# Reordering the norm loop, and changing how weight loads are guarded and cut, in a transformer layer on 8 cores

## The reference

```python
x = L0_attn_x                                   # [8, 4096, 1024] fp32
xn = _layernorm(x)
x = x + attention(xn) + ffn(xn)

# attention: 8 heads of 256, key and value from a latent of rank 64
q = xn @ Wq.T;  kv = xn @ Wkv_down.T
k = kv @ Wk_up.T;  v = kv @ Wv_up.T
out = softmax(q k^T / 16) v @ Wo.T

# ffn: weights rounded to {-1, 0, 1} by the mean of |w|, activations to 8 bits per token
gate = silu(bitlinear(xn, w_gate));  up = bitlinear(xn, w_up)       # 1024 -> 4096
y = bitlinear(gate * up, w_down)                                     # 4096 -> 1024
```

## Time and profile before

| what | value |
|---|---|
| runs | 5657.88, 6039.49 (median), 6048.05 us |
| the profiled execution | 5657.88 us, its span 5656.3 us (slowest core, core 6; cores 5638.6 to 5656.3) |
| granted PE clock | 0.890 to 0.891 of full speed on all cores |
| norm loop | 0 to 758 us |
| attention | 758 to 3491 us: PE busy 2314.15 us |
| first hole | 3491 to 3651 us: PE busy 12.87 us |
| up and gate | 3651 to 4862 us |
| second hole | 4862 to 5008 us: PE busy 28.78 us |
| down | 5008 to 5656 us: PE busy 636.40 of 648 us |
| busy over the span | PE 74%, DVE 37%, ACT 38%, POOL 12% |

### The profile page before, as it was taken

One profiled execution on the slowest core, in us unless ns is written; L12 is line 12 of the kernel. 1 busy time (PEld: TensorE's weight loads), 2 busy tenths in 40 slices (PEclk: granted clock), 3 DMA queues, 4 the chain that ended last, 5 costly groups with the idle time before them and its releaser, 6 DMA issues.

```text
span 5656.3 us, 93209 instructions; the slowest of 8 cores (5638.6 to 5656.3 us)
## 1 busy us (share of the span) xinstructions
PE 4170.3 (74%) x23803; PEld 2339.4 (41%) x24244; DVE 2077.0 (37%) x2817; ACT 2163.8 (38%) x3587; POOL 664.0 (12%) x643
## 2 busy tenths in 40 slices
PE   1222379798897987979879796288888888279999
PEld 1111246455453554635546363144333433134444
DVE  5434621211212112121121211099999999301111
ACT  3322456364563645636456363033333333100000
POOL 1110000000000000000000000133333333000000
PEclk9999689899898998979989898699999999589999
DMA  5454421011010110101101212111111111245553
GB/s 130 128 127 121 121 62 42 25 42 46 22 42 25 42 46 22 42 25 42 46 21 44 83 44 66 37 31 36 38 38 31 36 38 36 72 135 130 131 131 105
DMA packets 532527, 350.66 MB, mean 62 GB/s; under 512 B 441824, under 2 KB 482784, under 8 KB 532000
## 3 DMA queue, kind: packets, MB, share of 16 engines
q1 hardware_dynamic: 467856, 155.24, 11.9%
q0 software_dynamic: 51248, 164.26, 10.3%
q10 hardware_dynamic: 12896, 25.17, 1.3%
HBM read 244.61 MB, written 109.05 MB: 63 GB/s over the span
## 4 chain that ended last, share of the span: by engine, by line
PE 54%; DVE 23%; issue 9%; DMA 6%; ACT 5%; SPq 1%; DVEq 1%; POOLq 1%; ACTq 0%; POOL 0%
PE psF L710 17%; PE psF L699 15%; PE psF L997 8%; PE psF L383 4%; DVE rsc L461 4%; DVE t L452 3%; DVE rsc L458 3%; PE psF L983 3%; DVE arB L464 2%; PE psF L875 2%; DVE smf L900 2%; PE psF L881 2%; ACT arB L723 1%; DVE rsc L455 1%; PE psT L760 1%
## 5 line engine op out<-in xcount | busy, mean ns | idle before, releaser
L704 ACT ACTIVATE arB<-psF 128x512 bf16<-128x512 f32 x2048 | 1210.1, 597 | 695.0 <-PE psF L699 459.7
L710 PE MATMUL psF<-arB 128*128 128x257 bf16 x8192 | 1271.7, 281 | 135.7 <-ACT arB L704 133.9
L699 PE MATMUL psF<-arB 128*128 128x512 bf16 x3841 | 1192.0, 393 | 34.9 <-DVE arB L426 20.7
L710 PEld LDWEIGHTS psF<-arB 128*128 128x128 bf16 x8192 | 788.2, 100 | 559.7 <-issue 196.6
L875 PE MATMUL psF<-arA,arB 128*128 128x512 bf16 x1958 | 518.4, 406 | 94.5 <-DMA arB<-xnqT_d 85.1
L881 PE MATMUL psF<-arB 128*128 128x512 bf16 x2042 | 485.0, 380 | 62.3 <-DMA arB<-wuT_d 62.0
L997 PE MATMUL psF<-arB,arA 128*128 128x512 bf16 x2009 | 447.9, 381 | 82.7 <-DMA arB<-wdT_d 80.7
L896 POOL TENSOR_TENSOR arC<-arC 128x512 f32<-128x512 f32 x256 | 417.9, 1632 | 770.2 <-ACT arC L893 770.2
L699 PEld LDWEIGHTS psF<-arB 128*128 128x128 bf16 x4096 | 412.1, 101 | 112.4 <-issue 29.1
L719 DVE RECIPROCAL smf<-psF 128x1 f32<-128x1 f32 x256 | 43.1, 168 | 1128.7 <-PE psF L710 1108.0
L888 ACT ACTIVATE arC<-psF,smf 128x512 f32<-128x512 f32 x256 | 175.7, 686 | 635.2 <-PE psF L881 635.2
(11 more groups left out here) (130 smaller groups left out, 3601.6 us busy)
## 6 DMA issues: line engine op xcount, KB each, us to landing
arC<-Wg POOLq DMA_DIRECT2D x64, 512.0 KB, 5.5
arC<-Wu POOLq DMA_DIRECT2D x64, 512.0 KB, 5.8
arC<-Wd POOLq DMA_DIRECT2D x64, 512.0 KB, 5.7
hqT_d<-p1b SPq DMA_DIRECT2D x32, 1024.0 KB, 6.2
arA<-hqT_d SPq DMA_DIRECT2D x32, 1024.0 KB, 9.5
arC<-x SPq DMA_DIRECT2D x32, 512.0 KB, 4.9
aoT_d<-arB SPq DMA_DIRECT2D x64, 256.0 KB, 2.1
arC<-x ACTq DMA_DIRECT2D x32, 512.0 KB, 6.1
```

The costliest lines, as they stand in the source:

```text
L699: p.add("tensor", lambda e, bi=bi, c=c, g=g, d2=d2: e.matmul(bank(g), kT[:, d2 * T + c * 128: d2 * T + (c + 1) * 128], qT[:, d2 * T + bi * ...
L704: p.add("scalar", lambda e, g=g, c=c: e.activation(pT[c % 3][:, :], bank(g), AF.Exp, bias=0.0, scale=ISCL), reads=[b_bank[g]], writes=[b_p ...
L710: p.add("tensor", lambda e, c=c, sub=sub: e.matmul(pv_ps(sub, 0, 257), pT[c % 3][:, sub * 128:(sub + 1) * 128], vA[:, c * 257:(c + 1) * 25 ...
```

## The change

Seven edits:

- In the norm loop `emit_xnq_out`, `emit_passA` and `emit_prep_tile` move from the end of the iteration to before x's transposes; the kv product becomes a function (`emit_kv`) and is done one iteration later, also before x's transposes. The k and v groups of head 0 therefore start one chunk later.
- The very last aoT_d store uses buffer 0 of `aoTh` instead of 1.
- The first two xnqT_d loads are guarded by kvT and `aoTh[1]` alone.
- Each wuT_d slice is loaded in two pieces of 256 columns, the first by ACT, the second by POOL; the up product waits for both.
- In up and gate all four transpose groups stand behind the eight slices.
- wdT_d is loaded in eight 1 MB pieces, and a down matmul waits for its own piece.
- The guard lists are rebuilt for the new buffers.

```diff
+            if tc >= 1:
+                emit_xnq_out(tc - 1)
+            for j in range(3 * tc, min(3 * tc + 3, len(passA))):
+                emit_passA(j)
+            for _ in range(3):
+                emit_prep_tile()
+            if tc >= 1:
+                emit_kv(tc - 1)
             tb = nb()
             (x's eight transposes)
             (copy into arA)
-            (eight kv matmuls of tc, copy into kvT)
-            if tc >= 1:
-                emit_xnq_out(tc - 1)
             round5(xn32[:, :], b_xn, p1b[:, bb * 1024:(bb + 1) * 1024], rq, sxv, b_sxv)
-            for j in range(3 * tc, min(3 * tc + 3, len(passA))):
-                emit_passA(j)
-            for _ in range(3):
-                emit_prep_tile()
         emit_xnq_out(NTC - 1)
+        emit_kv(NTC - 1)
...
-                    if pre_k and 4 * pre_k[0][1] + 3 < tc:
+                    if pre_k and 4 * pre_k[0][1] + 4 < tc:
...
-                    if pre_v and pre_v[0] < tc:
+                    if pre_v and pre_v[0] + 1 < tc:
...
-                pb = bi % 2
+                pb = 0 if (h == NH - 1 and bi == 7) else bi % 2
...
-        b_wu8 = [Buf() for _ in range(8)]
+        b_wu8h = [[Buf(), Buf()] for _ in range(8)]
+        xnq_guard = b_kvT.handover() + b_aoTh[1].handover()
...
         for isl in range(8):
-            tok = p.add("scalar" if isl % 2 == 0 else "gpsimd", (load 512 columns),
-                reads=[b_d["wuT"]], writes=[b_wu8[isl]], extra=guard_wu, dma=True)
+            for hf in range(2):
+                c0 = isl * 512 + hf * 256
+                tok = p.add("scalar" if hf == 0 else "gpsimd", (load 256 columns from c0),
+                    reads=[b_d["wuT"]], writes=[b_wu8h[isl][hf]], extra=guard_wu, dma=True)
...
-                extra=((guard_wu + ao_guard) if tc < 2 else ()), dma=True)
+                extra=(xnq_guard if tc < 2 else ()), dma=True)
...
-                        reads=[b_xnqst[bb], b_wu8[isl]], writes=[b_bank[gu]])
-                if tc >= 1 and isl in (6, 7):
-                    emit_trans_group(tc - 1, isl - 6)
+                        reads=[b_xnqst[bb], b_wu8h[isl][0], b_wu8h[isl][1]],
+                        writes=[b_bank[gu]])
...
-                emit_trans_group(tc - 1, 2)
-                emit_trans_group(tc - 1, 3)
+                for g_ in range(4):
+                    emit_trans_group(tc - 1, g_)
...
         for n_ in range(2):
-            p.add("gpsimd", (load 32 x 512 columns of wdT_d),
-                reads=[b_d["wdT"]], writes=[b_wd2[n_]], extra=guard_wd, dma=True)
+            for q_ in range(4):
+                p.add("gpsimd", (load 8 x 512 columns, rows q_ * 8 on),
+                    reads=[b_d["wdT"]], writes=[b_wd2[n_][q_]], extra=guard_wd, dma=True)
...
-                        reads=[b_hqst[bb], b_wd2[n_]], writes=[b_bank[dbk[n_]]])
+                        reads=[b_hqst[bb], b_wd2[n_][ic // 8]],
```

More of the change, by code:

```diff
@@ L513, in emit_xnq_out, with emit_kv @@
                 reads=[rs2], writes=[b_d["xnqT"]], dma=True)
+        def emit_kv(tc2):
+            for dc in range(NDC):
+                p.add("tensor", lambda e, dc=dc, tc2=tc2: e.matmul(
+                    bank(0)[0:LR, 0:128], wkvT[:, dc * LR:(dc + 1) * LR],
+                    xnT_sl(dc, tc2 * 128, 128),
+                    start=(dc == 0), stop=(dc == NDC - 1)),
+                    reads=[b_wkvT, b_arA], writes=[b_bank[0]])
+            p.add("vector", lambda e, tc2=tc2: e.tensor_copy(
+                kvT[:, tc2 * 128:(tc2 + 1) * 128], bank(0)[0:LR, 0:128]),
+                reads=[b_bank[0]], writes=[b_kvT])
         pre_q = [(oc_, ts__) for ts__ in range(8) for oc_ in range(2)]
@@ L807, in build_nc @@
         for isl in range(8):
[L808 to L813 removed]
+            for hf in range(2):
+                c0 = isl * 512 + hf * 256
+                tok = p.add("scalar" if hf == 0 else "gpsimd",
+                            lambda e, c0=c0: e.dma_start(
+                    out=arB[:, 0:32768].rearrange("pp (dc i) -> pp dc i", i=NI)[:, :, c0:c0 + 256],
+                    in_=wuT_d.rearrange("(dc pp) i -> pp dc i", pp=128)[:, :, c0:c0 + 256]),
+                    reads=[b_d["wuT"]], writes=[b_wu8h[isl][hf]],
+                    extra=guard_wu, dma=True)
             tok_wu = tok
@@ L924, in build_nc @@
         emit_hq_dma(NTC - 1)
-        b_wd2 = [Buf(), Buf()]
+        b_wd2 = [[Buf() for _ in range(4)], [Buf() for _ in range(4)]]
         b_wo2 = [Buf(), Buf()]
@@ L956, in build_nc @@
         for n_ in range(2):
-            p.add("gpsimd", lambda e, n_=n_: e.dma_start(
-                out=arB[:, 0:32768].rearrange("pp (ic n) -> pp ic n", n=D)[:, :, n_ * 512:(n_ + 1) * 512],
-                in_=wdT_d.rearrange("(ic pp) n -> pp ic n", pp=128)[:, :, n_ * 512:(n_ + 1) * 512]),
-                reads=[b_d["wdT"]], writes=[b_wd2[n_]],
-                extra=guard_wd, dma=True)
+            for q_ in range(4):
+                p.add("gpsimd", lambda e, n_=n_, q_=q_: e.dma_start(
+                    out=arB[:, 0:32768].rearrange("pp (ic n) -> pp ic n", n=D)[:, q_ * 8:(q_ + 1) * 8, n_ * 512:(n_ + 1) * 512],
+                    in_=wdT_d.rearrange("(ic pp) n -> pp ic n", pp=128)[:, q_ * 8:(q_ + 1) * 8, n_ * 512:(n_ + 1) * 512]),
+                    reads=[b_d["wdT"]], writes=[b_wd2[n_][q_]],
+                    extra=guard_wd, dma=True)
         for n_ in range(2):
```

18 lines of the change are left out of this document (2 added, 16 removed).

## The result

The changed kernel's profiled execution took 5689.92 us (span 5688.4, core 5) against 5657.88 before: +32.0 us. Over the runs the ratio is 1.0059, 95% interval 1.0045 to 1.0073. It is slower, clear of the scatter of the runs but by less than 2%; the forecast was 5710 (+52.5). Many executions of every kernel here take some per cent longer, with a lower granted clock on half of the cores or on all of them; the ratios, the fastest times and the cores that are read are of the others.

The account below looks back on a forecast made before the run. The norm loop was bound by a chain with no engine full, up and gate by DVE, down by PE, with two nearly idle holes between. Norm loop +56, first hole +1, up and gate 0, wdT_d -4.5: 5657.9 + 52.5 = 5710 us, range 5670 to 5745.

Parts of the forecast that it names:

- First hole, +1: Hole before up and gate: SP's wait train shrinks, POOL's stays, so the hole moves behind gate 0; +1 us (-3 to +6).
- Rival A: First hole really closes, POOL's 135 us being no train of waits: -82 us, 5628 us; chance 7%.
- wdT_d in eight, -4.5: Second hole, before down: matmuls start about 8 us after the issue and keep pace with the loads; -4.5 us (-6 to 0).
- Norm loop, first part, +79: Iterations 0 to 9, small tiles: kv, x's transposes, copy and rounding follow the third tile serially; +79 us (+68 to +85).
- Wq iterations, -10: Norm loop, five iterations with Wq tiles: stores and x's load move 1.8 us ahead; -10 us (-15 to -5).
- Iteration 10, +3: Norm loop iteration that ends with a Wq tile: +3 us.
- Wo, +4.5: Norm loop, three Wo iterations: DMAs bind, and copies and rounding fall into DVE's idle time; +4.5 us (0 to +6).
- Last part, -22: Norm loop iterations 19 to 31, no tiles: DVE's copies follow one another without waiting for PE; -22 us (-30 to -12).
- Up and gate, 0: Third transpose group 3.4 us later, covered by the 6.0 us the fourth waits for DVE; 0 (-8 to +8).
- Rival B: In up and gate PE comes late, waiting behind slice 7 for ACT's first copy: +78 us, 5788 us; chance 7%.
- Rival C: Norm loop's first part loses little, tile loads being early enough (8 us fall to 2): 5650 us; chance 8%.

Follow-up runs that it names:

- rest_only: The changed kernel with the norm loop of the kernel before: ratio 0.9993, fastest run 5647.2 us.
- half_train: The changed kernel with every second wait left out of POOL's two long lists, same events waited for: ratio 0.9826, fastest run 5554.2 us.
- x_with_tile: The changed kernel with x's load held back in early iterations to go out with the third tile's load: 5692.9 us.
- load4_before: The kernel before with four load buffers for the prep tiles instead of two: 5639.2 us.
- x_early_before: The kernel before with x's load issued one chunk ahead: 5594.4 us.
- round_first: The changed kernel with only the rounding put ahead of the prep tiles, kv and x's transposes and copy staying behind them: 5666.4 us.

## Why the prediction was right in sign and too large

- **First hole, +1: right within its range.** The step that SP's short list opens gate 0 and POOL's 2151 waits keep the rest shut came out to the microsecond (135.34 us). Up slice 2 starts 169.0 us after the last score matmul, before it was some 170.6: -2, inside -3 to +6. Rival A is refuted by `rest_only`, and the mechanism behind it by `half_train`.
- **wdT_d in eight, -4.5: right.** PE starts 7.95 us after POOL's issue (about 8 forecast) and is through tc = 0 some 5 us sooner counted from it; the issue itself came 1.5 us later, counted from the last gate matmul. By the page "DMA: Bandwidth & Descriptors" of the Trainium skill, section "Anatomy of one DMA — SWDGE (gpsimd) path", a 1 MB DMA by itself takes an estimated 4.4 us. From 5019.00 to 5035.28 five pieces arrive, 3.3 us each; before, 4 MB took 11.6 us, 2.9 us per MB. So the trace doesn't agree with pieces taken one after the other, each with its fixed part in full; a few tenths of a microsecond per piece are there.
- **Norm loop, first part, +79: this is the step that failed; measured +57.** The serial path behind the third tile was right to 0.01 us. Wrong was that the third tile would come as late after the fp32 normalise as before ("The load isn't issued earlier", and 7.9 us per iteration "since most of these loads bind PE"). It comes at 11.2 us instead of 13.3, and these 2.1 us in ten iterations are 21 of the 22 us. The load is indeed issued no earlier, but it takes less time to land: 3.1 us instead of 4.9 on the slowest cores, 2.6 instead of 4.7 on the mean of eight. I had put at nothing that the change also sends SP's store and x's load out 3 us sooner, away from the tile's load. x's load is 0.9 of these 2.1 us (`x_with_tile`); the rest stays open, the store being the likely cause. DVE is the smaller part. Its copies behind the rounding kept the tile from PE until 12.8 us even when the load was in time (`load4_before`), and the change removes that bound too. But with the loads landing as they did before, at 12.8 us on the mean, freeing DVE alone would have won some 0.2 us; with DVE as before, the earlier loads alone some 0.3 (both estimated from the table of landings above). It took both. The earlier trace rows named DVE for one iteration; I took 1.1 us from it for this one and nearly nothing for the others, and neither row nor median says when the load lands once its neighbours move.
- **Wq iterations, -10: failed; measured 0, and -1.3 on the mean of the cores.** I had x's load 1.8 us earlier. In iteration 12 the first Wq tile reaches PE 0.9 us later in the loop (10.5 us after L582; before 9.6), which leaves 0.9, and x takes 5.3 us to land instead of 3.9. Over the five iterations and all cores the tile is 1.1 us later, x's load 0.7 us earlier, and it takes 0.3 us longer to land. `x_early_before` shows that x alone bound before the change; after it the rounding ends last, or within 1.4 us of x, so little could be won in any case. Why the tile and x come later was not tried.
- **Iteration 10, +3: measured +1.0. Wo, +4.5: measured +5.6. Last part, -22: measured -21.2.** The gain came where it was expected, from copies that no longer wait for PE.
- **Up and gate, 0: right**, and by the cover named: the third group is late, but only by up to 1.8 us (3.4 forecast), and the 6.0 us of the fourth group's wait took it in. Rival B would have needed more than 6.
- **Rival C** (the tiles' loads are early enough) was partly right: the loads were not early enough to hide the path behind them, but earlier than I had them.

The sum in its own terms: 57.0 + 1.0 + 0 + 5.6 - 21.2 - 0.1 = +42.3 for the norm loop, instead of +56.

## What to carry to other kernels

When work moves within a loop over in-order engines, ask two things of each wait in the old trace. What would have ended it next if its releaser had come at once? And which transfers does the move send out at another time? A load's time to land is no constant of the load: here the same 16 KB took 4.7 us just behind a 256 KB store and a 512 KB load, and 2.6 us when these had gone out 3 us sooner. Put what waits for a transfer last and what needs none ahead of it, unless another engine waits for it (`round_first`). And where a dependence list is turned into waits, keep one per semaphore: by the fastest runs that was worth 3.8% in the kernel before and 3.4% in the changed one, more than every guard that was trimmed by hand.
